# Values matmuls of two attentions on 512 query columns every second unit, instead of 256 columns in every unit

## The reference

```python
# per head h, with q, k, v of 8 features each
p = jax.nn.softmax(q @ k.T * 8 ** -0.5, axis=-1)
o = p @ v
x = x + concat_heads(o) @ out_w.T + out_b
```

## Time and profile before

| | us |
|---|---|
| median of 3 runs (lowest, highest) | 2942.01 (2937.75, 2942.84) |
| the profiled execution | 2941.23 |
| its span, from first to last instruction | 2938.9 |
| PE busy in the span | 2746.6 |
| DVE busy | 2487.6 |
| ACT busy | 2065.5 |
| starts of the first and the last row maximum (L528), both attentions | 23.0, 1639.1 |

### The profile page before, as it was taken

The page is one execution under the profiler, slowest core; times in us unless marked ns, Lnnn a source line. Parts: engine busy times, 40 slices in busy tenths (PEclk is TensorE's granted clock), DMA queues, the critical chain, the costliest instruction groups (busy, mean ns, idle before and its releaser), DMA issues.

```text
span 2938.9 us, 58153 instructions
## 1 busy us (share of the span) xinstructions
PE 2746.6 (93%) x23145; PEld 1253.3 (43%) x23149; DVE 2487.6 (85%) x3270; ACT 2065.5 (70%) x3906; POOL 921.3 (31%) x1052
## 2 busy tenths in 40 slices
PE   8999999999999989999999999999888799878889
PEld 2222222235666622222222356666333265467655
DVE  8999999976777699999999767776899956899744
ACT  6999999976666569999999766665776423745232
POOL 1000000013444410000000134543487555299810
PEclk9999999999999999999999999999999999989999
DMA  2000000000000010000000000000000000000000
GB/s 96 6 17 17 17 17 17 17 9 1 2 1 2 2 55 10 16 16 16 16 16 16 13 1 1 2 2 25 4 1 0 10 1 1 1 1 1 1 1 15
DMA packets 29148, 33.62 MB, mean 11 GB/s; under 512 B 13195, under 2 KB 23438, under 8 KB 28622
## 3 DMA queue, kind: packets, MB, share of 16 engines
q1 hardware_dynamic: 28878, 29.92, 3.5%
HBM read 17.58 MB, written 7.34 MB: 8 GB/s over the span
## 4 chain that ended last, share of the span: by engine, by line
PE 65%; DVE 20%; ACT 8%; issue 4%; POOL 2%; DMA 0%; DVEq 0%; SPq 0%; POOLq 0%; PEldq 0%; ACTq 0%
PE banks L401 15%; PE banks L383 10%; DVE max_parts L528 7%; PE banks L376 5%; PE banks L1119 2%; PE banks L2147 2%; PE banks L2132 2%; PE banks L2134 2%; PE banks L1094 2%; PE banks L1028 2%; ACT probs L644 2%; DVE banks L2998 2%; DVE state_keys L2995 2%; PE banks L1137 2%; DVE banks L3000 2%
## 5 line engine op out<-in xcount | busy, mean ns | idle before, releaser
L528 DVE TENSOR_REDUCE max_parts<-banks 128x2 f32<-128x1024 f32 x1024 | 1170.4, 1215 | 10.7 <-PE banks L376 9.2
L644 ACT ACTIVATE probs<-banks 128x512 f32<-128x512 f32 x2048 | 1085.4, 600 | 58.9 <-PE banks L383 32.3
L383 PE MATMUL banks<-q_parts,k_parts 51*128 51x512 bf16 x2048 | 654.6, 385 | 4.9 <-ACT v_heads L603 1.5
L401 PE MATMUL banks<-probs,v_heads 128*9 128x256 f32 x8192 | 637.9, 383 | 8.2 <-ACT pv_copy L655 2.0
L376 PE MATMUL banks<-k_parts,q_parts 48*128 48x512 bf16 x2048 | 595.8, 385 | 9.5 <-DVE max_parts L528 6.2
L711 POOL CAST neg_max_parts<-neg_max 128x8 bf16<-128x8 f32 x64 | 12.9, 202 | 1121.8 <-DVE neg_max L533 1121.8
L383 PEld LDWEIGHTS banks<-q_parts,k_parts 51*128 51x128 bf16 x2048 | 151.4, 94 | 475.1 <-ACT probs L644 396.9
L401 PEld LDWEIGHTS banks<-probs,v_heads 128*9 128x9 f32 x8192 | 123.4, 88 | 382.2 <-issue 343.1
L1681 POOL TENSOR_TENSOR state_times_c<-state,c_row 128x1024 f32<-128x1024 f32 x63 | 148.0, 2354 | 89.8 <-ACT c_row L1997 53.9
L1875 DVE TENSOR_TENSOR_SCAN state<-banks,state_carry,state 128x512 f32<-128x512 f32 x128 | 157.3, 1270 | 6.5 <-ACT banks L1992 4.4
L2318 ACT ACTIVATE silu_a<-banks 128x512 f32<-128x512 f32 x80 | 47.7, 597 | 163.2 <-PE banks L2132 163.0
(11 more groups left out here) (527 smaller groups left out, 5014.7 us busy)
## 6 DMA issues: line engine op xcount, KB each, us to landing
outT_half<-pv_copy SPq DMA_DIRECT2D x248, 16.0 KB
prob_sums<-pv_copy SPq DMA_DIRECT2D x248, 2.0 KB
q_scratch<-qk_parts SPq DMA_DIRECT2D x8, 384.0 KB, 3.5
k_scratch<-qk_parts SPq DMA_DIRECT2D x8, 384.0 KB, 2.6
k_parts<-k_scratch SPq DMA_DIRECT2D x28, 96.0 KB
q_parts<-q_scratch SPq DMA_DIRECT2D x28, 96.0 KB
q_parts<-neg_max_rows SPq DMA_DIRECT2D x128, 3.0 KB
ffn_weights<-moe SPq DMA_DIRECT2D x1, 1928.0 KB, 7.3
```

Of the source, the lines that this page charges most:

```text
L383: nc.tensor.matmul(bank("exp", n, x)[:, :], K[p % 2][half_of(x, ROWS + PARTS), tile(t)], Q[p % 2][half_of(x, ROWS + PARTS), blk(j)], start ...
L401: i = nc.tensor.matmul(PVb[group:group + VD, cols], V[:, t + k, 2 * (s // NB) + x, :], PT[:, (n + k) % RING, x, cols], start=(t == 0 and c ...
L528: nc.vector.tensor_reduce(mxp[s % 2][:, :, u // NB, u % NB], Mb[m % 2].rearrange("p (x k) -> p x k", x=2), AX.X, ALU.max).then_inc(*maxed. ...
L644: nc.scalar.activation(PT[:, n % RING, x, :], bank("exp", n, x)[:, :], ACT.Exp, scale=float(HD) ** -0.5).then_inc(*exped.inc())
```

## The change

values loses its argument c. It is issued once per two units, at even steps n for the units n - 4 and n - 3, with all 512 query columns in each matmul. Before, it came at odd steps n for the columns 0 to 255 of units n - 3 and n - 2, and in the next step for columns 256 to 511. The counts that ACT waits for are halved. Nothing else moves.

```diff
-            def values(n, c):
+            def values(n):
                 s, t = n // STAGE, n % STAGE
-                cols = slice(256 * c, 256 * c + 256)
                 pe.wait_ge(v_copied, NB)
                 pe.wait_ge(evacuated, s)
                 pe.wait_ge(exped, 2 * (n + 2))
                 for x in range(2):
                     for k in range(2):
                         group = 32 * (2 * x + k)
-                        i = nc.tensor.matmul(PVb[group:group + VD, cols], V[:, t + k, 2 * (s // NB) + x, :], PT[:, (n + k) % RING, x, cols],
-                                             start=(t == 0 and c == 0), stop=(t == STAGE - 2), skip_group_check=True)
+                        i = nc.tensor.matmul(PVb[group:group + VD, :], V[:, t + k, 2 * (s // NB) + x, :], PT[:, (n + k) % RING, x, :],
+                                             start=(t == 0), stop=(t == STAGE - 2), skip_group_check=True)
                 i.then_inc(*valued.inc())
...
-                if n >= 3 and (n - 3) // 2 * 2 < UNITS_ALL:
-                    values((n - 3) // 2 * 2, (n - 3) % 2)
+                if n >= 4 and n % 2 == 0 and n - 4 < UNITS_ALL:
+                    values(n - 4)
...
             def exponential(n, x):
-                act.wait_ge(valued, 2 * ((n - RING) // 2 + 1))
+                act.wait_ge(valued, (n - RING) // 2 + 1)
...
             def evacuate(s):
-                act.wait_ge(valued, STAGE * (s + 1))
+                act.wait_ge(valued, STAGE // 2 * (s + 1))
```

## The result

The changed kernel takes 3047.5 us in the median of 6 runs, where the kernel before takes 2941.0 beside it: a ratio of 1.0359, 95% interval 1.0348 to 1.0370. It is slower by 106 us. The forecast was 3039, with 3012 to 3062. The profiled execution of after took 3050.4 us.

The account below looks back on a forecast made before the run. VectorE was taken to bound the kernel at 18.38 us a stage; the three-bank round makes it 20.06. 60 x 1.68 = 100.8, -5.2 at boundaries, +2.4 for tails: +98.0 on 2941.2, so 3039 us, range 3012 to 3062.

Parts of the forecast that it names:

- VectorE is the limit before, and PE's relief is worth nothing: Attention stages: VectorE fills 18.3 of 18.38 us, so the 0.22 us PE saves per pair of units gains nothing.
- The burst is 0.98 us: Merged values burst on TensorE: 4 x 0.213 us of columns plus 0.12 of switching, 0.98 us against 0.55 before.
- A round of 2.36 us through three banks sets the pace: Burst, transposed scores, exponential, bank reuse, next burst: 2.36 us per two units, above VectorE's 2.26.
- Turn and copy pairs: Once a stage each: the turned maximum adds 0.49 us (2.85), the copy of the values 0.69 (3.05), to 2.36.
- boundary waits: At head-pair boundaries PE waits for key and query rows from DMA; longer stages remove this, -5.2 us.
- The tail: Last 23 units of each attention, after the reductions end: +1.2 us each, bounds 0 and +3.
- The bubble: Repeating idle time on VectorE before the row maximum, absent before, expected to appear: some 100 us in all.
- Loop not closed: Rival: the matmul does not wait for the exponential, only the maxima's banks bind; about 2965 us, 7 in 100.
- faster: Rival: PE is relieved and VectorE stays fed, the round being under 2.26 us; about 2932 us, 4 in 100.
- no change: Rival: as with a fed VectorE, but the gain is lost at the copy; no measurable change, 3 in 100.
- maxima's own two banks: Rival round through the row maximum's two PSUM banks: 3.44 us against 3.39, over by 0.05; no separate chance given.
- clock should fall for good: Rival: the granted clock falls to 1.2 GHz and stays, 770 us more, about 3700 us; 2 in 100.

Follow-up runs that it names:

- five banks: Changed kernel, maximum scores for the first head of each pair only, the two freed PSUM banks added to the transposed-scores ring (five for three): 2943.8 us, ratio 1.0013.
- mark: Kernel before (256 columns, three banks) with maximum scores computed for the first head of each pair only: 2946.0 us, ratio 1.0020.
- two_halves: Changed kernel with each long values burst written as two halves of 256 columns back to back, 16 instructions instead of 8: 3051.5 us, ratio 1.0376.
- short_off_loop: Changed kernel with the x = 0 exponentials of even units cut to 256 of 512 columns: 3046.3 us, ratio 1.0361.
- copy_later: Changed kernel with the copy of the values behind exponential (n, 1) instead of between the two of its step: 3015.4 us, ratio 1.0257.
- short_on_loop: Changed kernel with the x = 0 exponentials of odd units cut to 256 of 512 columns from unit 8 on: 2983.6 us, ratio 1.0149.
- turn_after: Changed kernel with turn_max one step later, in an even unit and behind the values burst: 3026.6 us, ratio 1.0292.
- both_moved: Changed kernel with the values copy behind exponential (n, 1) and turn_max one step later behind the burst: 3002.8 us, ratio 1.0207.
- loads_first: Kernel before with SP's key and query loads for the next head pair ahead of the gathers of their step: 2935.6 us, ratio 0.9986.

## Why the prediction was right

- *VectorE is the limit before, and PE's relief is worth nothing.* Shown: with less work for VectorE a stage of the kernel before went from 18.38 to 18.14 us, and with five banks the long burst ended level with its mark (2943.8 and 2946.0). The next limit was nearer than the prediction's text lets one think: PE's 1.09 us a unit leave out the turn and the copy, and with them it is 18.14.
- *The burst is 0.98 us.* Measured 0.98, for either width. The estimate by the 2.5 ns per matmul of the Trainium skill (TensorE: Matmul & The Clock Gate, Back-to-back issue gap), 1.08 us, did not hold here: the burst was 0.98 us, and 16 instructions took no longer than 8.
- *A round of 2.36 us through three banks sets the pace.* Measured 2.37; each of its five terms was within 0.01 us of its row in the kernel before. The exponentials on and off the round, the maxima and the five banks each agree with it.
- *Turn and copy pairs.* Turn pair 2.86 (forecast 2.85), copy pair 3.06 (forecast 3.05). Moving the turn gave back 0.46 us a stage within a head pair, of the 0.49 charged; moving the copy gave 0.48 of its 0.69, which by the rows of that kernel is what this move can give. Its expectation was only 0.27, because the end of the exponential was placed 0.24 us too late.
- *The sum.* The term that was a little too small is the stage, 20.17 for 20.06 us, 60 x 0.11 = +6.6 us. The 0.01 us in each of eight pairs is 0.08 of it; 0.03 a stage stays open. The boundary waits are gone as forecast: the mean stage equals the single one.
- *The tail.* From the last reduction to the last exponential of the first attention it was 29.4 us (615.2 to 644.6) and is 30.6 (669.3 to 699.9): +1.2, as forecast. In the second it went from 29.4 to 31.0.
- *What was not foreseen.* The start of the first attention was 3 us longer: the second joined maximum comes at 65.5 us, before at 62.3 (see the last section). The rest of the program behind the second attention, untouched, differed by 3 us between the two profiled executions, which is within the spread of the runs. So of the 8 us between the forecast and the median the stages explain most.
- *The bubble.* It appeared: 75.2 us of idle time in front of L527, and 0.2 us from 100 to 600 us with five banks. This bears out the rule of the Trainium skill (Perfetto Trace Analysis, Optimization Strategy) that a repeating bubble on the engine that should be full can mean too little PSUM.
- *The signs that were off.* The row maximum sat idle 75.2 us by the view, not some 100, and in three printed places of a stage, not in front of most second reductions. The rest is spread over slightly later starts: 20.17 us less the 18.3 of VectorE's own work is 1.87 a stage. And the sign against the forecast, a clock under 1.00 between 60 and 600 us, was set too early: it was 0.50 from 60 to 62 us, and 1.00 from 64 to 600.
- *The rivals.* Loop not closed, faster and no change are refuted by the 2.37 us rounds. The maxima's own two banks are refuted by the stage that stayed at 20.17 us with half the maximum. That the clock should fall for good is refuted by 1.00 from 64 us on.

## What to carry to other kernels

Merging small bursts of one engine into rarer, longer ones saves switching, but every ring of buffers that other work goes round must now last through the longer burst. Write down the round (burst, first producer behind it, consumer, the producer that reuses the buffer, next burst) and compare it with the pace of the engine that is the limit; here 2.37 stood against 2.26 us for two units, though no engine had more to do. That alone would have made a stage 8 x 2.37 = 18.96 us, 0.6 more than before. Two thirds of the loss, 0.49 and 0.69 us of the 1.8 a stage, came from the two dear places. Where an order is written by hand, an extra use of the ring or a waiting instruction placed between two consumers costs its length once the ring sets the pace. Before, both places were there too, and VectorE ran its sixteen reductions through them without a break.

## What the hardware showed that was not expected

The granted clock fell earlier at the start of the first attention, and whether it does is not a matter of the change. Stretches of the kernel after:

```profile
45.00:62.00 17.00, 16.05 (x65) 4.93 (x64) 12.78 (x12) 8.82 (x17) 0.00 (x0) 0.50 0.13 47
330.00:600.00 270.00, 247.63 (x1728) 54.13 (x1727) 255.05 (x229) 229.74 (x456) 10.18 (x52) 1.00 0.06 15
```

From 45 to 62 us the clock is at 0.50 (1.2 GHz), where it was still 1.00 from 45 to 49 us and 0.50 from 52 to 55 before. Ahead of the fall PE ran the scores for the maxima and, between them, the projections of the values (L348: 24 matmuls of 128 columns from 41 to 49 us before); the prediction's "only scores run" overlooked these. That part was not changed. Kernels that share it with the changed one went both ways: in two_halves, short_off_loop and copy_later the clock was 0.50 from 45 to 49 us, in short_on_loop, turn_after and both_moved 1.00. In loads_first, which shares it with the kernel before, it did not fall from 36 to 66 us. In the second attention the start took 39.8 us from the first reduction (1101.0) to the second joined maximum (1140.8), where it had taken 40.7. So this is a few us that can fall either way, and the 3 us here are not put down to the change. What makes it fall in one execution and not in another no run here shows.
